# Splitting the expert matrices in the order in which their first slots come up

## What is computed

```
bitlinear(x, w) = quantise(rmsnorm(x)) @ ternary(w).T       # int8-like rows, weights in -1, 0, 1
i = silu(bitlinear(x, Wi)) * (1 - f);  f = sigmoid(bitlinear(x, Wf));  g = bitlinear(x, Wg)
h_t = f_t * h_(t-1) + i_t                                   # a scan along the 512 tokens
x = layernorm(x + bitlinear(rmsnorm(g) * g_weight * silu(h), Wo))
e = min(token_id // 6250, 3)                                # one of 4 experts for each token
x = layernorm(x + (silu(x @ C[e].T) * (x @ C[e].T)) @ C[e]) # C = ctx_2048, used for gate, up and down
x = layernorm(x + (x @ sum over r of factors[r]) / sqrt(8) + bias)
```

## Time and profile before

| | |
|---|---|
| median of 3 runs (lowest, highest) | 368.54 us (367.43, 371.08) |
| profiled execution: time, span | 365.52 us, 363.7 us |
| mean granted TensorE clock, share of full | 0.928 |
| busy over the span: PE, DVE, ACT, POOL | 284.2, 224.8, 230.7, 200.4 us |

### The profile page before, as it was taken

One profiled execution on the slowest core, in us unless ns is written; L12 is line 12 of the kernel. 1 busy time (PEld: TensorE's weight loads), 2 busy tenths in 40 slices (PEclk: granted clock), 3 DMA queues, 4 the chain that ended last, 5 costly groups with the idle time before them and its releaser, 6 DMA issues.

```text
span 363.7 us, 5740 instructions
## 1 busy us (share of the span) xinstructions
PE 284.2 (78%) x1518; PEld 212.9 (59%) x1518; DVE 224.8 (62%) x488; ACT 230.7 (63%) x456; POOL 200.4 (55%) x381
## 2 busy tenths in 40 slices
PE   1277457575696797998998999498699999999950
PEld 1255225242474585776877677376488888888640
DVE  4699999999386669849856764433344444444420
ACT  3789877968366696877867766434455555555440
POOL 2465867758556257566746847534344444444542
PEclk9998759695599999999999999989999999999995
DMA  7999968762983621013002201201411111100000
GB/s 235 391 388 386 249 116 165 148 142 71 190 164 73 114 71 47 11 47 118 0 31 87 61 29 60 87 29 58 117 44 49 54 58 35 55 31 24 29 8 0
DMA packets 17406, 37.02 MB, mean 102 GB/s; under 512 B 1503, under 2 KB 1631, under 8 KB 17376
## 3 DMA queue, kind: packets, MB, share of 16 engines
q0 software_dynamic: 6496, 15.74, 18.6%
q1 hardware_dynamic: 10880, 20.92, 17.2%
HBM read 26.68 MB, written 10.76 MB: 103 GB/s over the span
## 4 chain that ended last, share of the span: by engine, by line
PE 36%; issue 8%; POOL 6%; ACT 6%; DVE 5%; DMA 5%; POOLq 0%; DVEq 0%; ACTq 0%; SPq 0%
PE bank_m L1316 4%; PE bank_m L1320 4%; PE bank_m L1317 4%; PE bank_z L1316 3%; PE bank_z L1317 3%; PE bank_z L1320 3%; DMA sorted_rows<-r,place 3%; PE bank_y L1316 3%; PE bank_y L1317 3%; PE bank_y L1320 3%; PE bank_tr L1285 2%; DMA rows<-sorted_rows 2%; PE bank_q L1285 2%; POOL n_d L313 2%; POOL x L353 1%
## 5 line engine op out<-in xcount | busy, mean ns | idle before, releaser
L312 POOL TENSOR_SCALAR n_v<-n_dev 128x1 f32<-128x1 f32 (+1 forms) x46 | 9.8, 214 | 66.1 <-ACT x L642 28.1
L1316 PE MATMUL bank_y<-c_hi,h_hi 128*128 x76 | 31.6, 416 | 3.5 <-issue 1.8
L1316 PE MATMUL bank_z<-c_hi,a_hi 128*128 x76 | 32.6, 429 | 2.2 <-ACT a_hi L610 2.0
L1316 PE MATMUL bank_m<-f_hi,m_hi 128*128 128x512 f32 x76 | 31.8, 419 | 1.7 <-ACT m_hi L610 1.7
L930 DVE TENSOR_TENSOR act_z<-bank_z,act_z 128x512 f32<-128x512 f32 x19 | 13.1, 691 | 32.2 <-ACT act_z L624 31.9
L1317 PE MATMUL bank_z<-c_lo,a_hi 128*128 x76 | 31.5, 414 | 0.0
L358 POOL DMA_INDIRECT out<-r,token_of x19 | 20.7, 1088 | 19.5 <-ACT r L649 16.4
L1317 PE MATMUL bank_y<-c_lo,h_hi 128*128 x76 | 30.1, 396 | 0.0
L1317 PE MATMUL bank_m<-f_lo,m_hi 128*128 128x512 f32 x76 | 30.1, 396 | 0.0
L313 POOL TENSOR_TENSOR n_d<-n_v,minus_half 128x1 f32<-128x1 f32 (+1 forms) x46 | 27.7, 603 | 3.8
L353 POOL TENSOR_TENSOR x<-x,bias_b 128x512 f32<-128x512 f32 x19 | 24.6, 1296 | 6.8 <-PE bank_q L1285 6.4
(11 more groups left out here) (205 smaller groups left out, 856.4 us busy)
## 6 DMA issues: line engine op xcount, KB each, us to landing
f_sum<-in_factors POOLq DMA_DIRECT2D x7, 1024.0 KB, 9.4
rows<-sorted_rows SPq DMA_DIRECT2D x19, 256.5 KB, 2.8
xs<-in_x SPq DMA_DIRECT2D x8, 512.0 KB, 6.5
c_stage<-in_ctx_t SPq DMA_DIRECT2D x4, 1024.0 KB, 14.3
sorted_rows<-pad_row SPq DMA_DIRECT2D x1, 1539.0 KB, 20.5
w_stage<-in_wf_t SPq DMA_DIRECT2D x1, 1024.0 KB, 8.9
w_stage<-in_wi_t SPq DMA_DIRECT2D x1, 1024.0 KB, 11.1
w_stage<-in_wg_t SPq DMA_DIRECT2D x1, 1024.0 KB, 13.2
```

What stands on the lines that cost most here:

```text
L1316: t.matmul(bank[:], hi[:, c, :], w_hi(c), start=(c == 0), stop=False)
```

## The change

Four things are done.

First, the split goes by pairs of chunks (128x1024, one instruction) and in another order: `rank_experts`, seven small VectorE instructions in turn 2, ranks the experts by their first slot into the tile expert_off, and `high_of_ctx(k, c)` and `low_of_ctx(k, c)` read the k-th expert's place from it into a register and address c_stage, c_hi and c_lo by that register.

Second, the pairs are made later: the first matrix around the end of turn 3, the second and third in turn 4, the fourth in turn 5 (the turns are counted from 0 here).

Third, `up(n)` waits for the split of the first n + 1 matrices of that order only; slot n can't need a later one.

Fourth, the orders on all four engines are rewritten up to slot 10. Turns 1 to 4 are written out step by step, the loop holds turns 5 to 7. The last loop, from slot 11 on, stays.

```diff
-                def high_of_ctx(e, chunks):
-                    act.wait_ge(s_ctx[e], 16)
...
-                    for c in chunks:
-                        a.activation(c_hi[:, KC * e + c, :], c_stage[:, KC * e + c, :], ACT.Copy).then_inc(s.hi, 1)
+                def high_of_ctx(k, c):
+                    if k == 0 and c == 0:
+                        for e in range(N_EXPERTS):
+                            act.wait_ge(s_ctx[e], 16)
+                            act.wait_ge(s.wready, e + 1)
+                            act.wait_ge(s.wready_pool, e + 1)
+                        act.wait_ge(s.expert_off, 1)
+                    at = act.value_load(expert_off[0:1, k:k + 1], min_val=0, max_val=(N_EXPERTS - 1) * KC)
+                    a.activation(flat(c_hi[:, bass.ds(at + c, PC), :]), flat(c_stage[:, bass.ds(at + c, PC), :]), ACT.Copy
+                                 ).then_inc(s.hi, 1)
...
-                def low_of_ctx(chunks):
-                    for c in chunks:
-                        dve.wait_ge(s.hi, c + 1)
-                        v.tensor_tensor(c_lo[:, c, :], c_stage[:, c, :], c_hi[:, c, :].bitcast(F32), ALU.subtract
-                                        ).then_inc(s.split_dve, 1)
+                def low_of_ctx(k, c):
+                    dve.wait_ge(s.hi, (KC * k + c) // PC + 1)
+                    at = dve.value_load(expert_off[0:1, k:k + 1], min_val=0, max_val=(N_EXPERTS - 1) * KC)
+                    chunks = bass.ds(at + c, PC)
+                    v.tensor_tensor(flat(c_lo[:, chunks, :]), flat(c_stage[:, chunks, :]), flat(c_hi[:, chunks, :]).bitcast(F32),
+                                    ALU.subtract).then_inc(s.split_dve, 1)
...
+                def rank_experts():
+                    dve.wait_ge(s.next_fill, 6)
...
+                    v.scalar_tensor_tensor(first_use[:], slot_at[:, 0, :], float(N_EXPERTS), expert, ALU.mult, ALU.add
+                                           ).then_inc(s.ranks, 1)
+                    dve.wait_ge(s.ranks, 1)
+                    v.tensor_tensor(pairs[:], first_use[:, :, None].to_broadcast(square),
+                                    first_use[:, None, :].to_broadcast(square), ALU.is_gt).then_inc(s.ranks, 1)
...
                 def up(n):
                     after(pe, s.hid, n)
+                    pe.wait_ge(s.split_dve, KC // PC * (min(n, N_EXPERTS - 1) + 1))
                     if n == 0:
-                        pe.wait_ge(s.split_dve, N_EXPERTS * KC)
```

More of the change, by code:

```diff
@@ L414, in _ @@
                 weight_ready(W_G)
+                places()
                 add_factor(1)
-                places()
                 scale_g(0)
                 power_x(2)
[L420 to L443, removed]
-                    number_rows(p)
@@ L446, in _ @@
[L446 to L452, removed]
+                scale_o(0)
+                power_x(3)
+                weight_ready(W_O)
+                number_rows(0)
+                scale_g(1)
+                add_factor(2)
+                power_1(0)
+                pool.wait_ge(s.padded, 16)
@@ new lines, in _ @@
+                max_o(0, 1)
+                scale_x(2)
+                rescale_i(1, 1)
+                quantise_x(2)
+                round_weights(W_O)
+                gate_i(1, 0)
+                quantise_o(0)
+                max_x(3, 0)
+                scans(1, 0)
+                weigh_g(1, 0)
+                gate_i(1, 1)
+                max_x(3, 1)
+                scans(1, 1)
+                weigh_g(1, 1)
+                residual_1(0)
+                rescale_f(2, 0)
+                rank_experts()
@@ new lines, in _ @@
+                output(1, 0)
+                output(1, 1)
+                rescale_f(2, 1)
+                rescale_i(2, 0)
+                max_o(1, 0)
+                scale_x(3)
+                max_o(1, 1)
+                quantise_x(3)
+                rescale_i(2, 1)
+                weigh_g(2, 0)
+                gate_i(2, 0)
+                quantise_o(1)
+                scans(2, 0)
+                gate_i(2, 1)
+                max_x(4, 0)
+                scans(2, 1)
+                residual_1(1)
@@ new lines, in _ @@
+                rescale_f(3, 0)
+                weigh_g(2, 1)
+                max_x(4, 1)
+                output(2, 0)
+                output(2, 1)
+                rescale_f(3, 1)
+                max_o(2, 0)
+                max_o(2, 1)
+                rescale_i(3, 0)
+                rescale_i(3, 1)
+                scale_x(4)
+                gate_i(3, 0)
+                quantise_x(4)
+                low_of_ctx(0, 0)
+                quantise_o(2)
+                scans(3, 0)
+                gate_i(3, 1)
@@ new lines, in _ @@
+                weigh_g(3, 0)
+                scans(3, 1)
+                weigh_g(3, 1)
+                residual_1(2)
+                output(3, 0)
+                low_of_ctx(0, 2)
+                max_x(5, 0)
+                rescale_f(4, 0)
+                max_x(5, 1)
+                low_a(0)
+                output(3, 1)
+                max_x(6, 0)
+                scale_x(5)
+                max_o(3, 0)
+                hidden(0)
+                rescale_f(4, 1)
+                max_o(3, 1)
@@ L1357, in _ @@
                 spread_max(1)
[L1359 to L1376 removed]
+                project_f(1)
```

589 lines of the change are left out of this document (364 added, 225 removed).

## The result

| | median us | range, runs | ratio to before (95%) |
|---|---|---|---|
| before, beside it | 369.80 | 367.43 to 371.08, 4 | |
| after | 344.17 | 343.18 to 345.69, 4 | 0.932 [0.925, 0.9385] |

The change takes 25.6 us off, 6.8%. The profiled execution of after took 344.6 us, span 342.6. Some executions of every kernel run about 1% or more longer at a lower mean granted TensorE clock, and the ratios leave them out. The mean granted clock of the profiled executions is 0.950 after and 0.928 before.

A forecast was written before the change was run, and what follows sets the result against it. VectorE was taken to bound the front, with TensorE's idle 21.8 us to win behind it. 6.3 + 2.0 + 1.3 + 3.0 - 1.5 = 11.1 us off 365.5, plus 3.0 to the median: 357.5 us, range 349 to 366.

The forecast's parts named there:

- Front 6.3 (4.7 to 8.3): Turns 0 to 3: splits out and ranking in win 6.3 us of VectorE's time, bounds 4.7 and 8.3.
- minus 2 for what they don't fill: Front: 2 us taken off for time the new order leaves unfilled where splits stood, bounds 0 and 3.6.
- Rival A: Front and seam: latency between VectorE, ScalarE and TensorE takes the splits' place, gain 7.8, so 360.7 us; chance 0.15.
- Seam 2.0: 94 to 103 us: silu_h_by_token(3) and project_f(4) fill TensorE's idle time, gain 2.0 us (0.3 to 3.8).
- turn 4 0 (3 either way): Turn 4: more VectorE work against a shorter wait for slot 1's rows, no change, bounds 3 us either way.
- Turn 5 0 (2 either way): Turn 5: two pairs on VectorE hidden by TensorE's work, no change, bounds 2 us either way.
- turns 6 and 7 1.3 (0 to 3): Turns 6 and 7: mix(n-3) ahead of transpose_a(n) shortens the wait for rows, 1.3 us of 3.4 idle.
- Stretch 3.0 (0 to 6): After turn 7: earlier oq_t and up(9) in the gap win 3.0 of TensorE's 10.5 us idle, bounds 0 to 6.
- Register loads 1.5: Eight new loads each on VectorE and ScalarE, taken at 0.2 us each, cost 1.5 us in all.
- Rival D: Register loads drain both queues, sixteen at 1.3 us are 20.8, kernel 8.2 us slower, 376.7 us; chance 0.06.
- Rival B: Turns 4 and 5: splits block GpSimd or add_factor(7) comes late, 6 us given back, 363.4 us; chance 0.14.
- Rival C: Behind the front: the rewritten order fills more of the idle 21.8 us, gain 19.6, 349 us; chance 0.15.

The follow-up runs named there:

- h1: Before with the new orders of turn 4, turns 5 to 7 and the stretch on all engines, old front, splits in turns 1 to 3: 346.89 us, ratio 0.936.
- f3: Before with turns 5 to 7 in their new order and GpSimd's power_x(6) of turn 4 moved ahead of power_1(3): 360.60 us, ratio 0.975.
- e1: Before with only the stretch after turn 7 in its new order, on all four engines: 360.56 us, ratio 0.974.
- f1: After with all its new orders, but the splits back in turns 1 to 3 and no ranking: 345.39 us, ratio 0.934 to before.
- e3: Before in its old order, with only the late paired splits and the ranking put in: 376.40 us, ratio 1.019.
- g4: Before with new turns 5 to 7 on ScalarE, VectorE and GpSimd and power_x(6) moved ahead, TensorE's turns 5 to 7 old: 370.56 us, ratio 1.000.
- e4: After with the experts' order written as constants, so no register loads on VectorE and ScalarE, ranking still computed: 343.42 us, ratio 0.928 to before.
- f4: After's front and turn 4, the last split at the end of turn 4, then old turns 5 to 7 and stretch: 366.29 us, ratio 0.994 to before.
- g2: After with GpSimd's weight_ready(W_O) moved ahead of power_x(3): 343.11 us, ratio 0.925 to before.
- f2: Before with one ScalarE step moved: o_by_channel(7) ahead of square_2(8) in the stretch after turn 7: 368.13 us, ratio 0.993.
- g3: Before with the new order of the stretch after turn 7 on TensorE alone: 366.54 us, ratio 0.989.

## Why the prediction was wrong

The direction was right, the size was not: 11.1 us forecast, 21 between the profiled executions and 25.6 between the medians. The step that failed is what the sum gave to the new orders behind the front. It had 0 for turn 4, 0 for turn 5, 1.3 for turns 6 and 7 and 3.0 for the stretch, 4.3 us with nothing for the clock; the runs show 6.1 for turn 4 with its seam (`h1`), 9.0 for turns 5 to 7 (`f3`) and 9.0 for the stretch (`e1`). The front, its largest term, came out smaller than forecast. So the places that it named for the profile were passed too late at first and too early at last: the end of `residual_1(2)` at 90.7 us (named: 86), `up(0)` at 95.2 (90), turn 5 at 122.6 (121), slot 11 at 241.9 (251). By its own steps:

- *Front 6.3 (4.7 to 8.3).* Measured 3.0 us (90.66 against 93.71), below the lower bound. The work removed was counted right: 8.7 us less VectorE work against 8.3 in the sum. A pair takes 1.22 us (taken: 1.15), a ranking step 0.20 (taken: 0.2). The failing term is "minus 2 for what they don't fill": 5.6 us, not 2, went into idle time of VectorE. Rival A's mechanism is what happened here, more strongly than it was priced, but not as its words have it: with the new orders VectorE is idle for 6.7 us of the front though the splits are there (`f1`), and with the old orders it is idle for 5.5 once they are gone (`e3`). Behind it, at `up(0)` and in turn 4, about half or more of what the late splits won was given back, a term that the sum didn't have.

```profile
56.05 0.15 DVE L1093 SCALAR_TENSOR_TENSOR first_use<-slot_at,small 128x4 f32<-128x4 f32 x1
56.24 0.17 DVE L1096 TENSOR_TENSOR pairs<-first_use 128x16 f32<-128x16 f32 x1
56.45 0.17 DVE L1099 TENSOR_REDUCE use_rank<-pairs 128x4 f32<-128x16 f32 x1
```

- *Seam 2.0 and turn 4 0 (3 either way).* Turn 4 failed. Turn 5 began 6.5 us earlier, of which 3.0 are the front's; the forecast for the seam had 2.0 more, and `up(0)` itself began only 0.8 us earlier. `h1` gives turn 4 with its seam 6.1 us by itself. The 2.6 us wait for the rows of slot 1 went, for the reason that the prediction gave. The prediction weighed VectorE's 24.0 us against TensorE's 20.6 in 25.8 and concluded that nothing was to be won; in after VectorE works 25.6 of the 27.4 us behind `up(0)`, and that part is still 5.6 us shorter than in before, with 2.7 us less of TensorE's idle time and 2.9 us of its work moved ahead.
- *Turn 5 0 (2 either way), turns 6 and 7 1.3 (0 to 3).* Measured 3.1 and 3.6 in the profiles, 9.0 by the medians of `f3`, above the upper bounds. I counted one wait, that for the rows, and not that the moved work also stands in the waits for act_z, xq_t and h_hi. Nearly all of TensorE's idle 6.1 us went, and `g4` shows that it doesn't go without TensorE's own new order.
- *Stretch 3.0 (0 to 6).* 7.4 in the profiles, 9.0 in `e1`. Of 10.5 idle us all but 4.7 went, and 1.6 us more came from the clock, which the sum didn't contain.
- *Register loads 1.5.* 0.8 us by the medians (`e4`), within the intervals nothing. Two of eight on VectorE show it idle by "issue", 0.77 us and 1.52 us, and the second stood ahead of the pair that `up(0)` waited for:

```profile
82.75 1.23 DVE L1028 TENSOR_TENSOR c_lo<-c_stage,c_hi  x1 [0.77 <-issue]
92.95 1.23 DVE L1028 TENSOR_TENSOR c_lo<-c_stage,c_hi  x1 [1.52 <-issue]
102.79 1.21 DVE L1028 TENSOR_TENSOR c_lo<-c_stage,c_hi  x1
```

  Of the eight pairs the other six show no idle time at all. At the place of the 1.52 us `f4` has 0.99 and `g2` 0.35, and `e4`, without the loads, none. The Trainium skill, page "Advanced Engine Details and Errata", section "Sequencer and Instruction Queues", says that other instructions can be read and queued while a control instruction executes. The six rows agree, the two don't, and no row shows how full the queue was. Rival D, which needs all loads exposed, is refuted by `e4`.
- *Rival B* (late splits give back in turns 4 and 5): it happened, by another road than GpSimd's. In after it is the 1.8 to 3.9 us above, at the seam and in turn 4; turn 5 takes 29.2 us in after and 29.1 in `f1`. In the old order it is more: in `e3` and `f4` splits stand ahead of a chain on VectorE or ScalarE, and turn 5 is 5.8 and 7.4 us longer than in before. GpSimd's blocking is there too, once 2.32 us for a step of 0.20 us, beside VectorE's four differences for the factors (129.84 to 132.3) and the pair at 132.25; TensorE's idle time in that turn is 0.4 us.
- *Rival C* (the order fills more of the idle 21.8 us, 349 us, chance 0.15) is the right mechanism; of TensorE's idle time behind the front 8.5 us are left in after (2.5 + 0.4 + 0.9 + 4.7). Its own terms for turn 4, turns 5 to 7 and stretch, 3 + 2 + 4 = 9, were 6, 9 and 9 by the ladder below. That its 349 us is the nearest number to 344.2 is in part luck: its 8.3 for the front and 3.8 for the seam didn't come. The forecast took the front as the main gain and the orders as extras; it is the reverse.

The ladder by medians: before 370; stretch and turns 5 to 7 353.0; turn 4 346.9; front 345.4; late splits with ranking 343.4; register loads 344.2. The last three steps are each about as large as their intervals.

`e1` and `f3` gain 9.0 each by the medians, while before and after differ by 7.4 and 6.7 in these sections of the profiles. The other profiles show why: that of before lies low. The eight with its code up to turn 5 (in three of them with `power_x(6)` moved) begin turn 5 at 129.1 to 131.5 us, before at 129.1. Of the four with its code up to the stretch, before begins it at 222.7 and `e1`, `f2` and `g3` at 224.4 to 226.2. From there to the end the old stretch and the last loop take 141.0 to 143.5 us in six profiles, 141.0 in before, and with the new stretch 132.3 to 134.4 in ten. What stays open is what makes one execution of the same code shorter than another; the rows of slot 0 above are one place.

## What to carry over

Where an engine that is nearly full stands idle in many small waits (here 21.8 of 159 us), price a reordering by all of that idle time, plus what the lower clock costs there, and not by the one wait that you can name. An order is one thing across engines: TensorE's alone lost 2.8 us in turn 4, the feeders' alone gained nothing in turns 5 to 7, one GpSimd step in its old place took back 7.5 us; so look at each join for what the first instruction of a new section needs and what stands ahead of its maker. Work taken off the busiest engine comes back only as far as its neighbours are early: of 8.7 us, 3.0 came back at the end of the front, and the late splits by themselves gave the whole kernel 1 to 2.

## What the chip showed beside that

- A 1024-column split takes VectorE 1.22 us and ScalarE 1.06. Back to back, two pairs take VectorE 2.35 us against 2.49 for four instructions of 512 columns (`f1`, before), and ScalarE 1.98 against 2.17 (both in `f4`): pairing saves about 0.1 us a pair on either.
- TensorE's matmuls of 0.39 us took 0.63 for 2 to 3 us behind 3.5 us of idle time in before (granted clock 0.96 over the stretch), and for 3.4 us in `g3` behind 1.30 and 0.33 us; behind a wait of 1.5 us later in before's stretch they were at 0.40 at once. In `f2` behind 1.85 us, and at the seam of after behind 2.07, they took 0.39 to 0.40 at first, until 1.8 and 1.3 us after the wait, and only then 0.63; behind 1.54 us at the same seam in `f4` they stayed at 0.39. So the lower clock can come in rows that show no wait, and the length of the wait just ahead doesn't tell whether it comes.
- The rows of slots 1 and 2 (256 KB each) landed 2.6 to 3.0 us after their issue where `add_factor(6)` (1 MB) came behind them, and 6.9 to 9.2 us where it had been issued 2.9 to 4.7 us before.
- In eleven profiles with the same old front `residual_1(2)` ended at 93.2 to 95.1 us, and in eight turn 5 began at 129.1 to 131.5. So single profiles don't tell differences under some 2 us; after's 90.7, with 91.1 and 91.5 in `f4` and `e4`, lies outside.
